# Marking the meeting cell of a DTW back-track: nine one-slot comparisons against premultiplied order numbers in two instructions

## The reference

```python
def _dtw_cost(D):                       # D is 64 x 512: distances
    row0 = jnp.cumsum(D[0])
    ...                                 # R[i,j] = D[i,j] + min(R[i-1,j], R[i,j-1], R[i-1,j-1])
def _backtrack(R, T1, T2):
    ...                                 # from (63, 511): argmin(diagonal, up, left) until (0, 0)
def _align_one(small, large):
    D = _pairwise_euclidean(small, large)
    R = _dtw_cost(D)
    i_idx, j_idx, valid = _backtrack(R, T_small, T_large)
    contrib = small[i_idx] * valid[:, None].astype(small.dtype)
    return jnp.zeros((T_large, d), dtype=small.dtype).at[j_idx].add(contrib)
...
x = x + _L0_xattn_ref(ctx_1024, _layernorm(x, axis=-1))
x = x + _L0_ffn_ref(_layernorm(x, axis=-1), w1, b1, w2, b2)     # 256 -> 1024 -> 256, 8-bit steps
```

## Time and profile before

| | |
|---|---|
| median of 3 runs | 191.33 us (191.01 to 192.35) |
| the profiled execution | 191.8 us |
| its span, first to last instruction | 189.9 us |
| VectorE busy | 154.4 us (81%) |
| TensorE busy (matmul) | 101.5 us (53%) |
| ScalarE busy | 101.8 us (54%) |
| granted TensorE clock, mean | 0.789 of full speed |
| outside the span | 1.9 us (191.8 less 189.9) |

### The profile page before, as it was taken

The page is one execution under the profiler, slowest core; times in us unless marked ns, Lnnn a source line. Parts: engine busy times, 40 slices in busy tenths (PEclk is TensorE's granted clock), DMA queues, the critical chain, the costliest instruction groups (busy, mean ns, idle before and its releaser), DMA issues.

```text
span 189.9 us, 3733 instructions
## 1 busy us (share of the span) xinstructions
PE 101.5 (53%) x1239; PEld 68.4 (36%) x1239; DVE 154.4 (81%) x754; ACT 101.8 (54%) x183; POOL 37.6 (20%) x97
## 2 busy tenths in 40 slices
PE   0789951000270000000001977978999999998991
PEld 0779850000140000000000333644666666665671
DVE  1994866999999999999998089797989989996351
ACT  3776766299991000044050009677686867777720
POOL 8964463000000000000000000002222405132250
PEclk9999997555555555555555599999999999999998
DMA  5993004800079500020112420004417354472847
GB/s 180 349 348 122 7 5 140 332 0 0 5 250 337 187 0 0 0 71 0 69 69 76 61 34 11 3 0 55 51 13 105 42 74 58 54 79 40 105 56 168
DMA packets 19603, 16.89 MB, mean 89 GB/s; under 512 B 5760, under 2 KB 19200, under 8 KB 19456
## 3 DMA queue, kind: packets, MB, share of 16 engines
q1 hardware_dynamic: 14336, 12.69, 20.7%
q0 software_dynamic: 3808, 3.67, 15.9%
q10 hardware_dynamic: 1440, 0.30, 0.8%
HBM read 7.48 MB, written 9.18 MB: 88 GB/s over the span
## 4 chain that ended last, share of the span: by engine, by line
DVE 46%; PE 40%; ACT 4%; issue 4%; DMA 3%; DVEq 0%; SPq 0%
PE y L1225 12%; PE h L1208 6%; DVE Y L1008 6%; DVE R L801 5%; PE t L1208 3%; DVE A L769 3%; DVE enter L995 3%; DVE bcarry L994 3%; PE e L1169 3%; DVE carry L789 3%; DVE M L790 3%; PE h L1121 3%; DMA X<-in_x_dram 3%; PE y L1238 2%; PE t L1121 2%
## 5 line engine op out<-in xcount | busy, mean ns | idle before, releaser
L466 POOL DMA_DIRECT2D out_dram<-E x14 | 17.0, 1217 | 137.2 <-DVE E L980 137.2
L1225 PE MATMUL y<-w2T,XT 128*128 128x256 bf16 x256 | 37.7, 273 | 0.4 <-DVE XT L970 0.4
L1238 PE MATMUL y<-w1T 128*128 128x512 bf16 x19 | 6.7, 513 | 46.6 <-DVE S_lo L1022 46.6
L1225 PEld LDWEIGHTS y<-w2T,XT 128*128 128x128 bf16 x256 | 25.0, 98 | 14.7 <-DVE XT L970 0.7
L616 ACT ACTIVATE h_int<-h,b_s 128x512 int16<-128x512 f32 x37 | 25.4, 686 | 5.6 <-PE h L1208 5.0
L1208 PE MATMUL h<-M,w1T 128*128 128x512 bf16 x74 | 21.9, 380 | 1.7 <-ACT M L609 1.6
L1238 PEld LDWEIGHTS y<-w1T 128*128 128x128 bf16 x19 | 2.1, 123 | 50.1 <-DVE S_lo L1022 46.9
L622 ACT ACTIVATE code<-Y,shifts 128x640 bf16<-128x640 bf16 x3 | 2.5, 828 | 32.5 <-DVE enter L995 32.5
L970 DVE TENSOR_SCALAR XT<-h_int 128x1024 bf16<-128x1024 int16 x28 | 12.1, 439 | 9.0 <-ACT h_int L616 9.0
L1158 PE MATMUL t<-ident_bf,w_raw 128*128 128x128 bf16 x32 | 4.6, 312 | 22.6 <-ACT w_raw L561 21.0
L616 ACT ACTIVATE h_int<-t,b_s 128x512 int16<-128x512 f32 x19 | 13.0, 686 | 3.1 <-PE t L1208 2.9
(11 more groups left out here) (195 smaller groups left out, 266.5 us busy)
## 6 DMA issues: line engine op xcount, KB each, us to landing
X<-in_x_dram SPq DMA_DIRECT2D x8, 512.0 KB, 8.2
out_dram<-b_s SPq DMA_DIRECT2D x7, 512.0 KB, 5.5
out_dram<-E POOLq DMA_DIRECT2D x14, 256.0 KB, 4.3
w_raw<-in_L_ffn_w_dram SPq DMA_DIRECT2D x2, 1024.0 KB, 5.9
S<-in_ctx_dram SPq DMA_DIRECT2D x1, 512.0 KB, 3.8
out_dram<-E SPq DMA_DIRECT2D x4, 128.0 KB, 2.7
path_dram<-A SPq DMA_DIRECT2D x3, 160.0 KB, 1.8
path_dram<-XT SPq DMA_DIRECT2D x3, 160.0 KB, 1.9
```

What stands on the lines that cost most here:

```text
L466: nc.gpsimd.dma_start(tiles_out[:, b:b + 2, quad_of(g), :], res[:, g % 2, 2 * h:2 * h + 2, :], accum_op=ALU.add).then_inc(out_stored[g % 2 ...
L1225: mm = nc.tensor.matmul(bank67[t // 2][:, t % 2, :], hq[:, g % 2, n, t * P:t * P + P], w2T[:, n, :], start=(n == 0 and not bias), stop=(n ...
L1238: nc.tensor.matmul(bank67[0][:, :, :].rearrange("p j d -> p (j d)"), w1T[:, 0, 0:P], w1T[:, 0, 0:512], start=True, stop=True)
```

## The change

`start_slots` is gone. While the forward pass begins, ScalarE multiplies the order numbers with each of the nine mask columns and writes nine copies, `order_own`; this stands behind `S_mid` and ahead of the weights, and waits for `step_done` to be 1. VectorE compares these copies with `start` itself. Slot 39 is marked ahead of the first scan, as before; the other eight are marked by one instruction over 8 x 65 = 520 columns behind the first scan. The first marking also waits for the nine ScalarE instructions. `back_count` follows the new number of increments.

```diff
-        start_slots = sb("start_slots", [P, CH + 1])
+        order_own = sb("order_own", [P, CH + 1, W + 1])
...
+        own_marked = sem("own_marked")
...
         def back_count(lo):
-            return 2 + 4 * (SLOTS - lo) + max(0, SLOTS - max(lo, HR))
+            return 3 + 4 * (SLOTS - lo)
...
             act.wait_ge(ctx_rest, 1)
             nc.scalar.activation(S_mid[:, :, :], S_r1[:, :, :], ACT.Copy).then_inc(ctx_split, 1)
+
+            act.wait_ge(step_done, 1)
+            for k in range(CH + 1):
+                nc.scalar.activation(order_own[:, k, :], order_back[:, :], ACT.Copy,
+                                     scale=own_slot[:, k:k + 1]).then_inc(own_marked, 1)
...
             signal(diagonal(HR + 5))
-            link(nc.vector.tensor_scalar(start_slots[:, :], own_slot[:, :], start[:, :], None, ALU.mult))
             signal(diagonal(SLOTS - 1))
             signal(diagonal(HR + 6))

-            def start_at(k):
-                return nc.vector.scalar_tensor_tensor(out=NL_start[:, k, :], in0=order_back[:, :], scalar=start_slots[:, k:k + 1],
-                                                      in1=NL_more[:, k, :], op0=ALU.not_equal, op1=ALU.mult)
+            def start_at(lo, hi):
+                return nc.vector.scalar_tensor_tensor(out=NL_start[:, lo:hi, :], in0=order_own[:, lo:hi, :], scalar=start[:, :],
+                                                      in1=NL_more[:, lo:hi, :], op0=ALU.not_equal, op1=ALU.mult)
...
-            start_at(CH).then_inc(back_done, 1)
+            v.wait_ge(own_marked, CH + 1)
+            start_at(CH, CH + 1).then_inc(back_done, 1)
             steps_of(SLOTS - 1).then_inc(back_done, 1)
...
-                if s >= HR:
-                    start_at(s - HR).then_inc(back_done, 1)
+                if s == SLOTS - 1:
+                    start_at(0, CH).then_inc(back_done, 1)
                     n += 1
```

## The result

| | before | changed |
|---|---|---|
| median of 20 runs each | 191.86 us | 191.00 us |
| ratio, 95% interval | | 0.9948, 0.9928 to 0.9967 |
| profiled execution / its span | 191.8 / 189.9 us | 189.99 / 188.2 us |

The change makes the kernel 0.5% faster: 0.0052 x 191.86 = 1.0 us (0.6 to 1.4 by the interval), where 1.10 was forecast. The level is 0.8 above the forecast of 190.2, most of it because the median of before, 191.33 with three runs, is 191.86 with twenty. Runs more than 1.5% above the fastest of the same kernel count in no ratio; of the changed kernel's twenty that is one, at 316 us.

What follows compares the result with a forecast made beforehand. VectorE alone was taken to set the time from about 36 to 103 us. The terms -0.26 - 1.57 + 0.67 + 0.06 gave -1.10 us (bounds -1.62 to -0.95), so 191.33 would become 190.2 us, range 189.2 to 191.3.

Steps and rivals of the forecast that it cites:

- Step 1 and 4: VectorE ahead of the first scan: removing `start_slots` saves 0.26 us; a second semaphore at the first marking adds 0.06.
- Steps 2 and 3: VectorE's back pass: eight narrow markings leave the rounds, -1.57 us; one wide marking behind the first scan adds 0.67.
- The lower bound of the sum: Total shift on VectorE's path with the wide marking at 0.23 us and no extra wait: -1.62 us.
- Step 5: ScalarE ahead of the weights: nine copies take 2.2 us, done at 38.1, cover over 20 us, cost 0.
- Step 6: `back_count` and after: ScalarE's pieces, stores and path loads move with VectorE; from `S_lo` everything is earlier by the same amount.
- Rival A and B: Clock around the first alignment: A, rises earlier, 189.5 or 188.4 us, chance 0.10; B, rises later, 192.1 us, chance 0.05.
- the same rise 5.8 us behind the start: Sign to look for: the clock rises some 5.8 us behind TensorE's start, as before.
- Rival C: Back pass: the wide marking costs more than the line; 1.77 us would lose the gain, milder case 190.8; chance 0.12.

Runs made afterwards that it cites:

- wide twice: Changed kernel with the wide marking issued a second time into a spare tile; median of the nine counted runs 191.17 us, ratio 0.994.
- clock early: Changed kernel with 14 idle TensorE matmuls from slot 7 of the back pass and 14 instead of 10 behind `S_lo`; median 189.57 us, ratio 0.9884.
- GpSimd marks: Changed kernel with VectorE marking only slots 39 to 37 and GpSimd the other six; median 191.83 us, ratio 1.0.
- before with the early clock: Kernel before with 14 idle TensorE matmuls from slot 7 of the back pass and 14 behind `S_lo`; median 190.59 us, ratio 0.9915.
- nine narrow: Changed kernel with eight slots marked by eight narrow instructions in the rounds, from the premultiplied numbers; median 191.44 us, ratio 0.996.
- one of nine: Changed kernel with one marking for all nine slots (585 columns) ahead of the first scan; median 190.80 us, ratio 0.9912.
- both: Changed kernel with one marking for all nine slots and the early idle TensorE matmuls together; median 189.69 us, ratio 0.9853.
- copies later: Changed kernel with ScalarE's nine copies waiting for the 130th increment of `step_done` instead of the first; median 190.80 us, ratio 0.9929.
- copies late: Changed kernel with ScalarE's nine copies waiting for the 65th increment of `step_done` instead of the first; median 190.84 us, ratio 0.9936.
- changed, again: Changed kernel run again unmodified, compared with the kernel before on the same chip; median 190.95 us, ratio 0.9931.

## Why the prediction was right

**Step 1 and 4, `start_slots` and the second semaphore.** -0.26 + 0.06 was forecast, -0.27 measured, in all eight executions that have the new tail within 0.01 us. The extra wait costs nothing here: it is the mis-sized term of the sum. The price came from a shuffle whose two waits were taken to be long met. The marking waits for the last flag row anyway and begins 0.03 us behind its end (72.09 against 71.56 + 0.50), as with one semaphore before (0.04).

**Steps 2 and 3, the merging.** -1.57 + 0.67 = -0.90 forecast, -0.89 measured. The rounds without marking are 0.72 us, the wide marking lasts 0.75 us against 0.76 and costs 0.68 against 0.67. At 585 columns it costs 0.75, 0.07 us for 65 columns more. By the rule of 58 cycles and one per column in the Trainium skill ("VectorE: DVE Perf Modes", section on the TRN2 errata) an estimate for 520 columns is 0.60 us. That is too low here by its fixed part, as the narrow ones already said, and the section itself says that this row predicts too little for single instructions; its slope agrees. The lower bound of the sum, printed as -1.62, adds up to -1.60.

**Step 5, the copies.** 2.27 us for nine against 2.2; no delay of the weights. The cover was put at over 20 us; it is longer than that, since 22 us of delay cost nothing. I had expected the bias stores to end it and they did not. The times named for the copies, the first scan and TensorE's start were missed, because this execution reached M 0.65 us later; the distances held.

**Step 6.** From the scan of slot 31 to `S_lo` 23.06 to 23.08 us in all profiled executions of the table. The step's other claim, that the path loads move with VectorE, did not hold: on ScalarE's queue they began 1.35 to 1.78 us behind `S_lo` in the seven executions that mark slot 39 ahead of the first scan and the others together behind it (the changed kernel twice, wide twice, both late copies, clock early, GpSimd marks), and 0.77 to 0.82 in the five others (before, before with the early clock, nine narrow, one of nine, both). The large store landed 2.4 to 2.9 us behind its issue in the seven and 1.9 in the five. Whether the change does this, and how, was not tried and stays open. It costs nothing where the ten idle matmuls end later than the loads land. Where the clock rose earliest (copies later) the alignment waited for the loads until 5.04 us behind `S_lo`, some 0.1 behind the last idle matmul, and with the early clock it costs about 0.3 us.

**Rival A and B, the clock.** The mechanism is real. In the executions without an edit on TensorE the stretch from `S_lo` to X follows the moment at which the granted clock rises, counted from the start of `S_lo` (worked out from the granted clock of windows of 0.5 us):

| | rise behind `S_lo` | `S_lo` to X |
|---|---|---|
| before | 7.1 | 7.16 |
| wide twice | 6.9 | 7.13 |
| copies late | 6.5 | 6.93 |
| GpSimd marks | 5.2 | 6.35 |
| nine narrow | 5.0 | 6.21 |
| one of nine | 4.9 | 6.17 |
| changed | 4.3 | 5.86 |
| changed, again | 4.3 | 5.86 |
| copies later | 3.9 | 5.92 |

With the early matmuls the stretch is 5.28 to 5.61, and the medians fall by 1.4 us. But the clock did not decide this change: with the wide marking the rise comes anywhere from 3.9 to 6.9 us behind `S_lo` (for the kernel before there is one trace, which can't show its spread), and with the rise put early in both kernels the trace still shows 1.16 us between them at `S_lo`, and 0.82 at X. The profiled execution of before was a late one, that of the changed kernel an early one, so the two profiles alone overstate the change by 1.3 us in that stretch and understate it by 0.65 ahead of M.

The rise is not tied to the start of TensorE's work. With the same ten matmuls it came 5.8 us behind that start before, 3.0 in the changed kernel, and 2.7 to 5.7 in the others of the table above. The forecast's sign "the same rise 5.8 us behind the start" was wrong for that reason. The Trainium skill ("TensorE: Matmul & The Clock Gate", Part 1) says that the activity watch runs free of the kernel's start. By that rule such a spread is to be expected, and the traces agree.

**Rival C**: excluded by the stretches. The wide marking costs 0.68 us where the loss of the gain wanted 1.77, and nothing behind it is slower up to `S_lo`.

**The level.** The forecast of 190.2 missed the measured 191.0 by 0.8: 0.5 of it is the median of before at three runs against twenty, the rest the 0.1 of the shift and the spread of the draw.

What made the stretch from 0 to M vary, by 1.9 us without the execution with the wide marking twice and by 3.0 with it, was not tried and stays open. The chain there has waits of TensorE with no releaser in the profile in several executions, of other lengths each time.

## What to carry to other kernels

Price a short VectorE instruction by the difference between rounds with it and without it, not by its duration: 0.20 us on the path for a duration of 0.28 here, of which 0.13 is fixed, so merging eight of them behind one precomputed operand saves seven fixed parts. When the expected gain is smaller than the spread between runs, cut the profiled span at named instructions on both sides of the edit: the stretch with the edit repeats to 0.02 us while whole runs move by 1.8. And where an engine sits idle before a stage that it bounds, look at what clock it begins with: on the kernel before, idle matmuls started some 5 us ahead of `S_lo`, with four more behind it, brought 0.9% (0.5 to 1.2), at least as much as the whole change (0.5%, 0.3 to 0.7).

## What the hardware showed that I had not expected

- An extra semaphore wait at an instruction that waits for another one anyway cost 0.00 us: from `start` to the first scan the removed step came back whole, 0.27 us for the 0.26 priced. The one pair of rows at shuffles had 0.08 us more with a second wait.
- A GpSimd instruction of 390 f32 columns takes 1.69 us, and a short VectorE instruction beside it 0.47 us in place of 0.20; a VectorE scan beside the 0.93 us one that follows takes 0.89 in place of 0.35.
- Even at the upper clock level the first alignment starts 4.4 to 4.7 us behind the start of `S_lo`, not the 3.8 expected: in the kernel before and in the last run at about the end of the 14 matmuls (4.41 and 4.55), in the changed kernel with the early clock alone at the landing of its loads (4.73).
